# Layer 1 of a fused two-layer attention kernel: from one row a period to two rows a period, with projections of 512 columns

## What is computed

```python
x = x + _L1_conv_ref(_gn(x), pair_repr, gate_proj, qkv_proj, out_proj, bias_proj)

def _L1_conv_ref(msa_repr, pair_repr, gate_proj, qkv_proj, out_proj, bias_proj):
    # msa_repr: 1 x 128 x 256 x 256 (rows s, positions r, channels), 8 heads of 32 channels
    bias = jnp.einsum('nijz,zh->nhij', pair_repr, bias_proj)[:, None]
    gate = jax.nn.sigmoid(msa_repr @ gate_proj).reshape(bs, s, r, head, c)
    q, k, v = jnp.split(msa_repr @ qkv_proj, 3, axis=-1)
    sim = jnp.einsum('nsqhc,nskhc->nshqk', q, k) * scale
    sim = jax.nn.softmax(sim, axis=-1)
    sim = sim + bias
    attend = jnp.einsum('nshqk,nskhc->nsqhc', sim, v) * gate
    return attend.reshape(bs, s, r, cm) @ out_proj
```

## Time and profile before

| | |
|---|---|
| median of 3 runs | 4790.2 us |
| profiled execution, its own time | 4786.58 us |
| span of its trace (first to last instruction) | 4784.8 us |
| mean granted TensorE clock over the span | 0.976 |
| TensorE matmul busy | 4548.7 us, 95% |
| VectorE busy | 3951.4 us, 83% |
| ScalarE busy | 3860.5 us, 81% |
| GpSimd busy | 3617.1 us, 76% |
| DMA | 383 MB, mean 80 GB/s |

### The profile page before, as it was taken

One profiled execution on the slowest core, in us unless ns is written; L12 is line 12 of the kernel. 1 busy time (PEld: TensorE's weight loads), 2 busy tenths in 40 slices (PEclk: granted clock), 3 DMA queues, 4 the chain that ended last, 5 costly groups with the idle time before them and its releaser, 6 DMA issues. The chain is left out here.

```text
span 4784.8 us, 154166 instructions
## 1 busy us (share of the span) xinstructions
PE 4548.7 (95%) x46135; PEld 3884.5 (81%) x46135; DVE 3951.4 (83%) x12976; ACT 3860.5 (81%) x11664; POOL 3617.1 (76%) x6054
## 2 busy tenths in 40 slices
PE   4557999999999999999999979999999999999998
PEld 1225888888888888888888868888999888888887
DVE  5443999989999999999999968888888888888887
ACT  2326999989999899989998968888888888888886
POOL 3443888888888888888888837777777777777776
PEclk8778999999999999999999989999999999999999
DMA  9996111111111111111111111111111111111111
GB/s 358 355 347 195 60 56 61 53 62 53 61 53 61 53 61 53 61 53 62 56 58 55 59 36 55 53 53 52 49 51 52 53 53 53 53 53 53 53 53 35
DMA packets 237388, 383.13 MB, mean 80 GB/s; under 512 B 18756, under 2 KB 156616, under 8 KB 224968
## 3 DMA queue, kind: packets, MB, share of 16 engines
q1 hardware_dynamic: 237256, 381.63, 23.6%
HBM read 309.21 MB, written 72.35 MB: 80 GB/s over the span
## 5 line engine op out<-in xcount | busy, mean ns | idle before, releaser
L1539 POOL TENSOR_SCALAR l_probs<-l_probs,l_inv 128x256 f32<-128x256 f32 x2048 | 941.5, 479 | 377.1 <-DVE l_inv L1436 377.1
L664 POOL TENSOR_SCALAR l_probs<-l_probs,l_inv 128x256 f32<-128x256 f32 x2048 | 951.1, 478 | 287.3 <-DVE l_inv L947 287.3
L865 ACT ACTIVATE l_probs<-l_probs,l_neg_max 128x256 f32<-128x256 f32 x2048 | 1016.0, 499 | 20.8 <-DVE l_neg_max L939 13.8
L1337 ACT ACTIVATE l_probs<-bank,l_neg_max 128x256 f32<-128x256 f32 x2048 | 942.5, 476 | 46.2 <-DVE l_neg_max L1430 39.4
L939 DVE CUSTOM_DVE_ANT_0 l_probs<-bank,bias 128x256 f32<-128x256 f32 x2048 | 785.2, 421 | 117.8 <-issue 83.3
L1443 DVE TENSOR_TENSOR l_probs_t<-bank,bias 128x512 f32<-128x512 f32 x1024 | 669.7, 686 | 130.8 <-PE bank L1249 115.9
L1430 DVE TENSOR_REDUCE l_neg_max<-bank 128x2 f32<-128x512 f32 x1024 | 675.0, 682 | 43.1 <-PE bank L1237 33.9
L1249 PE MATMUL bank<-ident,l_probs 128*128 128x128 f32 x4096 | 559.8, 274 | 5.3 <-POOL l_probs L1539 3.9
L799 PE MATMUL bank<-ident,l_probs 128*128 128x128 f32 x4096 | 546.1, 276 | 9.7 <-DVE l_probs_t L961 7.4
L799 PEld LDWEIGHTS bank<-ident,l_probs 128*128 128x128 f32 x4096 | 450.2, 141 | 109.2 <-issue 106.8
L817 PE MATMUL bank<-l_probs_t,l_v 128*64 128x256 f32 x4096 | 498.5, 385 | 0.4
(11 more groups left out here) (205 smaller groups left out, 14578.1 us busy)
## 6 DMA issues: line engine op xcount, KB each, us to landing
fp_x<-in_x_dram SPq DMA_DIRECT2D x32, 1024.0 KB, 6.5
fp_ln_w<-in_L_conv_ln_w_dram SPq DMA_DIRECT2D x32, 1024.0 KB, 8.8
fp_ln_b<-in_L_conv_ln_b_dram SPq DMA_DIRECT2D x32, 1024.0 KB, 11.3
fp_pair<-in_L_conv_pair_repr_dram SPq DMA_DIRECT2D x32, 1024.0 KB, 11.2
l_x<-in_x_dram SPq DMA_DIRECT2D x128, 256.0 KB, 2.9
l_ln_w<-in_L_conv_ln_w_dram SPq DMA_DIRECT2D x128, 256.0 KB, 3.3
l_ln_b<-in_L_conv_ln_b_dram SPq DMA_DIRECT2D x128, 256.0 KB, 3.5
x<-l_y SPq DMA_DIRECT2D x128, 256.0 KB, 2.0
```

Of the source, the lines that this page charges most:

```text
L664: last = nc.gpsimd.tensor_scalar(probs[:, h, c], probs[:, h, c], inv[:, h, c:c + 1], 1.0, ALU.mult, ALU.mult)
L865: last = nc.scalar.activation(probs[:, h, c], probs[:, h, c], ACT.Exp, bias=neg_max[:, h, c:c + 1], scale=-1.0, accum_out=total[:, h, c:c ...
L1337: last = nc.scalar.activation(probs[:, h, c], b_s[h % 4][:, c * W:(c + 1) * W], ACT.Exp, bias=neg_max[:, h, c:c + 1], accum_out=total[:, h ...
L1539: last = nc.gpsimd.tensor_scalar(probs[:, h, c], probs[:, h, c], inv[:, h, c:c + 1], 1.0, ALU.mult, ALU.mult)
```

## The change

Layer 1 now handles two rows ("a pair") a period, 64 pairs in all:

- `xn`, `q`, `kk_` and `gate` have both rows side by side. `by_weights` makes one half j of the channels for both rows in 2 x 3 = 6 matmuls of 512 columns, and `queries`, `keys` and `gates` are called twice a pair, for j = 0 and 1. Their bank is emptied by one instruction of 128 x 512 elements for each j, as it was for each row before.
- `values`, `project_out`, `attend`, `scores`, `transposes`, `turn` and all of the softmax are called as often as before, for row r of the pair, with the same shapes.
- `probs`, `probs_t`, the maxima, sums and inverses have a buffer for each row of the pair.
- The order of each engine is a new list, with up to five pairs in flight, and the table R_BANK says which of the two shared banks a step uses.
- A class `Turns` works out the semaphore counts from a list of steps and how many pairs ahead they are.
- The loop body holds two pairs; one body before the loop and four behind it stand outside.
- Weights and biases of layer 0 are freed before layer 1, which makes room for the larger buffers.

```diff
+class Turns:
+    def __init__(self, pairs, turns):
+        self.pairs, self.turns = pairs, turns
+    def count(self, p, *which):
...
-    UNROLL, BUFS = 4, 4
-    AHEAD = 5
+    ROWS, UNROLL, BUFS = 2, 2, 4
+    PAIRS = C0 // ROWS
+    AHEAD, ENDS = 5, 4
...
-    TURNS = (1, 2, 3, 0, 5, 4, 7, 6)
+    QUERIES = Turns(PAIRS, [(0, 4), (1, 3)])
+    SCORES = Turns(PAIRS, [((1, 0), 2), ((1, 1), 2), ((0, 0), 3), ((0, 1), 3)])
...
+    R_BANK = {("AV", 0): 0, ("AV", 1): 1, ("G", 0): 0, ("G", 1): 1, ("K", 0): 0, ("K", 1): 0, ("OUT", 0): 0, ("OUT", 1): 0, ("Q", 0): 1, ("Q", 1): 1, ("V", 0): 1, ("V", 1): 1, ("tn", 0): 0, ("tn", 1): 1}
...
-        xn = [sb("xn_high", [P, 2, HC, W], F32R), sb("xn_low", [P, 2, HC, W], F32R)]
+        xn = [sb("xn_high", [P, 2, HC, ROWS, W], F32R), sb("xn_low", [P, 2, HC, ROWS, W], F32R)]
...
-        k_whole = sb("k_whole", [P, HC, W])
-        probs = sb("probs", [P, NH1, KC, W])
+        k_whole = sb("k_whole", [P, ROWS, W])
+        probs = sb("probs", [P, ROWS, NH1, KC, W])
...
             def by_weights(bank, weights, k):
 
-                for j in range(HC):
-                    for c in range(HC):
-                        last = matmul_split(nc, bank[:, j * W:(j + 1) * W], [weights(part, c, j) for part in range(2)], [x_[:, k % 2, c] for x_ in xn],
-                                            start=c == 0, stop=c == HC - 1)
+                for c in range(HC):
+                    last = matmul_split(nc, bank[:], [weights(part, c) for part in range(2)], [x_[:, k % 2, c].rearrange("p r c -> p (r c)") for x_ in xn],
+                                        start=c == 0, stop=c == HC - 1)
                 return last
...
+            def attend(t, k, r):
+                p = UNROLL * t + k
+                pe.wait_ge(t_ready, BIASED.count(p, *((r, h) for h in range(NH1))))
+                if r == 0:
+                    bank = 0
+                    if exists(p - 1):
+                        pe.wait_ge(v_ready, VALUES_OUT.count(p, 0))
+                        pe.wait_ge(y_ready, RESIDUALS.count(p - 1, 0))
...
+            def gates(t, k, j):
+                p = UNROLL * t + k
+                pe.wait_ge(x_ready, X_LOW.count(p, 0, 1))
...
+                else:
+                    bank = 1
+                    if exists(p - 2):
+                        pe.wait_ge(o_ready, GATED.count(p - 2, 1))
...
-        m.bias0 = sb("bias0", [P, KC, NH0, W])
+        early = ctx.enter_context(ExitStack())
...
+        m.bias0 = early.enter_context(nc.sbuf_tensor("bias0", [P, KC, NH0, W], F32))
...
+        early.close()
         layer1(nc, m, x1, out)
```

More of the change, by code:

```diff
@@ L78, in over_rows @@
         loop_ends_peeled(engine, total // unroll, body, hinted, ends)
+class Turns:
+    def __init__(self, pairs, turns):
+        self.pairs, self.turns = pairs, turns
+    def count(self, p, *which):
+        if isinstance(p, int) and p < 0:
+            return 0
+        counts = []
+        for place, (turn, ahead) in enumerate(self.turns):
+            if turn in which:
+                more = [other - ahead + (at <= place) for at, (_, other) in enumerate(self.turns)]
+                counts.append(sum(min(max(p + n, 0), self.pairs) for n in more) if isinstance(p, int) else sum(more))
+        return max(counts) if isinstance(p, int) else len(self.turns) * p + max(counts)
 class Chain:
@@ L1099, in layer1, with pairs @@
         block = ctx.enter_context(nc.Block())
-        def count(s, h, order):
-            return NH1 * s + order.index(h) + 1
-        def rows(engine, row):
-            over_rows(engine, C0, UNROLL, row, ahead=AHEAD, behind=1, ends=2)
+        def pairs(engine, pair):
+            over_rows(engine, PAIRS, UNROLL, pair, ahead=AHEAD, behind=1, ends=ENDS)
         @block.sync
@@ L1299, in row @@
                 if has(0):
[L1300 to L1301 removed]
+                    project_out(t, k, 0)
                 if has(1):
[L1303 to L1312 removed]
@@ L1328, in _ @@
-            rows(pe, row)
+                    transposes(t, k + 1, 1, 6)
+                if has(4):
+                    queries(t, k + 4, 0)
+                if has(1):
+                    transposes(t, k + 1, 1, 4)
+                    attend(t, k + 1, 0)
+                if has(2):
+                    scores(t, k + 2, 1, 1)
+                if has(1):
+                    transposes(t, k + 1, 1, 5)
+                if has(3):
+                    queries(t, k + 3, 1)
+                if has(4):
+                    keys(t, k + 4, 0)
@@ new lines, in pair @@
+                if has(2):
+                    transposes(t, k + 2, 0, 1)
+                    transposes(t, k + 2, 0, 0)
+                if has(3):
+                    values(t, k + 3, 0)
+                if has(2):
+                    transposes(t, k + 2, 0, 3)
+                if has(0):
+                    project_out(t, k, 1)
+                if has(3):
+                    scores(t, k + 3, 0, 0)
+                if has(1):
+                    attend(t, k + 1, 1)
+                if has(2):
+                    transposes(t, k + 2, 0, 2)
@@ L1514, in row @@
-                if has(-1):
-                    residual(t, k - 1)
-            rows(dve, row)
+                    biased_out(t, k + 1, 1, 7)
+                    biased_out(t, k + 1, 1, 4)
+                if has(2):
+                    inverse(t, k + 2, 1, 0)
+                    inverse(t, k + 2, 1, 3)
+                if has(4):
+                    queries_low(t, k + 4, 0)
+                if has(2):
+                    inverse(t, k + 2, 0, 4)
+                    maxima(t, k + 2, 1, 5)
@@ L1563 @@
+            pairs(pool, pair)
 class Memory:
```

994 lines of the change are left out of this document (658 added, 336 removed).

## The result

The changed kernel takes 4803.7 us in the median of 12 runs (4800.2 to 4806.0); the kernel before took 4790.9 on the same chip (12 runs). The ratio is 1.0026, 95% interval 1.0018 to 1.0035: slower by 13 us. I had forecast 4763, faster.

What follows compares the result with a forecast made beforehand. TensorE, busy without a gap, was taken to bound the kernel. 64 x (0.81 - 0.18) = 40 us saved and 13 given back at the ends make -27, from 4790.2 to 4763 us; range 4738 to 4815.

Steps and rivals of the forecast that it cites:

- Fewer, wider matmuls: Layer 1's queries, keys and gates: 36 matmuls of 512 columns replace 72 of 256, saving 0.81 us a pair (0.43 to 0.90).
- R1: Rival: the excess is a cost of each matmul, 0.226 us for 512 columns; time 4787; chance 0.12.
- The order on TensorE: Layer 1: two more projection groups a pair begin behind a transpose, at 0.09 each, costing 0.18 us (0 to 0.36).
- Everything else per pair, new waits: Layer 1's other work unchanged and other engines hidden, zero; waits for late-read banks priced zero, upper end 0.5 us a pair.
- both tight places: VectorE must finish row 1's `gated` before gates 1, margin 0.8 us, and row 0's residual before attend 0, margin 0.6.
- R2: Rival: TensorE waits once a pair for a bank VectorE reads late; 1 us a pair gives 4827; chance 0.18.
- Start and end: Layer 1's start costs +7 us and its end +6, together +13, ends +4 and +22.
- R3: Rival: layer 1's ends cost +30 instead of +13, with ten rows in flight; time 4780; chance 0.07.
- Everything ahead of layer 1: unchanged.: Before layer 1: freeing memory costs no instruction, so zero; span's start to first turn forecast to change by 0.

Runs made afterwards that it cites:

- e4: The changed kernel with queries, keys and gates made by 72 matmuls of 256 columns again instead of 36 of 512: 4824.3 us.
- e7: The changed kernel with another start of layer 1: pairs 1 and 2 turned in the transposes' free banks, ScalarE rounding row 1 earlier: 4797.4 us.
- e8: The changed kernel with another end of layer 1: row 1's projection ahead of one group of transposes, last five reciprocals ahead of the residual: 4803.2 us.
- e3: The kernel before, with only its memory placed as in the change: 4800.3 us.
- e5: The changed kernel with layer 0's weights moved 192 bytes and all behind them in layer 0 256 bytes: 4796.5 us.
- e6: The kernel before with layer 0's weights moved 64 bytes and everything behind them 256 bytes: 4801.7 us.
- e10: e5 with layer 1's normalised rows and all row buffers behind them 64 bytes further on: 4785.8 us.
- e14: The kernel before with layer 1's normalised rows and all buffers behind them 64 bytes further on: 4767.3 us.
- e13: e9 with e10's shift in layer 1 and 64-byte shifts of layer 0's keys, softmax, values and outputs: 4772.5 us.
- e17: e14 with layer 0's keys, softmax, values and outputs also shifted by 64 bytes against their partners: 4762.3 us.
- e9: The changed kernel with e5's placement, e7's start and more reordering of both ends, projections going ahead of transposes at the end: 4783.4 us.
- e18: e14 with 192 bytes instead of 64 in front of layer 1's normalised rows: 4768.2 us.
- e15: The changed kernel with the gates' matmuls on only the first 64 columns of each block of weights (output not the reference's): 4804.9 us.

## Why the prediction was wrong, by its steps

*Fewer, wider matmuls*: the failing step. "I take 0.2155" measured 0.230, above my upper end of 0.226. I had taken the nearest row by width, groups whose matmuls pass their columns twice with another type; there the excess all but vanishes, in this stream it grows. 0.81 us a pair became 0.30 (e4), 33 us less over 64 pairs. The Trainium skill (TensorE: Matmul & The Clock Gate, Back-to-back issue gap) gives columns divided by 2.4 plus 2.5 ns, for an isolated matmul; the trace disagrees with it at both widths, 0.119 and 0.230 where it has 0.109 and 0.216. R1 had the direction, and by its count 16 us.

*The order on TensorE*: priced 0.18 us a pair; e4 shows -0.02 for the whole order. I charged 0.09 for the slow first matmul behind a transpose and missed that the transpose ahead of it is 0.08 shorter, so a switch is free. This error of 13 us went the other way and hid a part of the first one.

*Everything else per pair, new waits*: right. No matmul waits, TensorE is busy all of the steady stretch, so both tight places had the time they needed. R2 did not occur. The pair's 29.87 lies inside the band of 29.2 to 30.1 that I gave for "not wrong", against 29.5 forecast. Both terms together: 20 us saved, 40 forecast.

*Start and end*: +28 measured, +13 forecast, +22 was my upper end. At the start I counted matmuls ahead of the first scores and took the chains as covered; TensorE waited 10 us in four places (the rows above) for banks and for the one buffer, and e7 takes 6.3 of them back. At the end I counted GpSimd's divisions, 17.3 us, and they took 19.5; but behind them stand transposes, additions and two outputs through one buffer, at a clock that has fallen, and e8 shows that earlier divisions alone win nothing. R3 named the size (+30) and got 0.07.

*Everything ahead of layer 1: unchanged.* I didn't price it, because "freeing memory costs no instruction". True, and it still cost 8.7 us (e3), recovered in e5, reproduced in e6. Without it the change still stands at +4 us by e3 and at +5 by e5, whose interval (2 to 11 us slower) leaves out no change, though barely. So the placement is most of the 13 us, but the sign comes from the width as well: a saving of 0.81 us a pair would have covered both.

For the profiled execution the measured parts add up to 3 (first pass) + 10 (layer 0) + 15.7 + 12.5 - 23.6 = 17.6, against 17.4. Of the 44 us by which this misses my -27, 16 lie in the steady part (33 too much for the width, less 13 for the order and 3 elsewhere), 15 at the two ends and 13 ahead of layer 1.

Is the change worth having? With both kernels placed well it is not: e10 4785.8 against e14 4767.3. A pair gains only 0.12 us there, 8 us in all, against 28 for longer ends. Even with its ends shortened (e13, 4772.5) it stays 10 us behind e17.

## What to carry to other kernels

When a change frees or reorders memory, check where operands lie in all stages that it didn't touch: compare the pace of an untouched stage (here 9.127 against 9.16 us) before anything else is explained. A deeper pipeline's fill and drain are chains of single buffers and shared banks, and are priced by following them in order of time, not by counting what runs more. Shortening one engine's part of such a chain can win nothing (e8, where TensorE's clock was also low for longer); e9, which moves waiting work of TensorE into the hole, kept the clock and shortened the end. And a switch between two kinds of matmul is priced by both distances at it, the last of the one kind and the first of the other.

## What was not expected of the hardware

- With weights and rows 64 bytes apart modulo 128, two rows of matmuls of 256 columns take 0.36 to 0.38 us less: one that moves w_v takes 0.113 us instead of 0.12 (e14). It is worth 24 us in 4791. A shift of 32 bytes loses, 192 wins as much as 64 but at other matmuls (e18), and at 512 columns there is next to no gain (e10). By what mechanism, and which operands count, no run here shows.
- At 1.2 GHz matmuls of 256 and 512 columns take exactly their columns' time, 0.213 us and 0.427; at 2.4 GHz the same streams take 12 ns more for 256 columns and 17 for 512, and halving the weights read changes that by 1.4 ns (e15).
- A projection's first matmul behind a transpose takes 0.20 us instead of 0.119, and the transpose ahead of it 0.03 instead of 0.109: the switch costs nothing (before, e4).
- In the drain of e8, six heads' transposes ran at half clock behind 5 us in which TensorE was busy for 2.1; in e9 the work behind 5 us with 3.25 busy ran at full clock.
